# Rebuilding the head of a token, attention and expert kernel: bias exponentials, layer norm, load order and TensorE's order

## The reference, cut to what matters

```python
h = tok_embedding[x] + position_row                 # (2, 2048, 64)
a = layernorm(layernorm(h)) * ln1_g + ln1_b         # both norms, then q, k, v
q, k, v = split(a @ qkv_w + qkv_b, 3)
attn = softmax(q @ k.T + bias_table[m - n + 2047 clipped to 1022]) * scale
h = h + layernorm(attn @ v @ proj_w + proj_b) * ln2_g + ln2_b
g = layernorm(h);  top 2 of 8 experts by g @ Wg + bg + bias
h = h + sum over the two of weight * (relu(g @ W1[e] + b1[e]) @ W2[e] + b2[e])
```

## Time and profile before

| | us |
|---|---|
| median of 3 runs | 143.33 |
| the three runs | 142.25, 143.33, 146.63 |
| the profiled execution, its span from first to last instruction | 143.1 |
| DVE busy | 113.6 (79%) |
| PE busy | 106.9 (75%) |
| POOL busy | 71.6 (50%) |
| ACT busy | 59.4 (42%) |

### The profile page before, as it was taken

How to read it: one execution, slowest core, us unless ns; L and a number is a source line. 1 busy time by engine, 2 the same in 40 slices (tenths; PEclk the granted TensorE clock), 3 DMA queues, 4 the chain that set the end, 5 groups by cost and what they waited for, 6 DMA issues and landing times.

```text
span 143.1 us, 2799 instructions
## 1 busy us (share of the span) xinstructions
PE 106.9 (75%) x1029; PEld 61.7 (43%) x1029; DVE 113.6 (79%) x339; ACT 59.4 (42%) x114; POOL 71.6 (50%) x85
## 2 busy tenths in 40 slices
PE   0007655999989999999959759759747959729980
PEld 0003343459448547734623433625422446327650
DVE  6599999893955177169999998998999999999623
ACT  3005600210020464369968942647946625620020
POOL 2059991502620286256968993549399830360000
PEclk9999999999755558659999996986997576896555
DMA  3785000000000000000000000001000001004021
GB/s 82 285 321 216 0 0 0 0 5 1 5 0 0 0 0 0 0 2 7 0 0 7 0 0 0 5 5 32 0 5 2 0 8 33 0 0 110 5 73 37
DMA packets 5397, 4.45 MB, mean 31 GB/s; under 512 B 4515, under 2 KB 4743, under 8 KB 5256
## 3 DMA queue, kind: packets, MB, share of 16 engines
q1 hardware_dynamic: 5162, 4.18, 9.0%
q10 hardware_dynamic: 222, 0.10, 0.4%
HBM read 3.21 MB, written 1.06 MB: 30 GB/s over the span
## 4 chain that ended last, share of the span: by engine, by line
PE 44%; DVE 43%; issue 5%; DMA 3%; ACT 2%; POOL 1%; SPq 0%; DVEq 0%; ACTq 0%; POOLq 0%
PE bank L909 9%; DVE acc L818 6%; PE bank L1060 5%; PE bank L1080 4%; DVE prod L811 4%; PE bank L991 3%; DMA vec<-in_vecs_dram 3%; PE bank L988 3%; DVE xs L777 3%; PE bank L1075 2%; PE bank L1085 2%; DVE oneh_j L639 2%; DVE xs L776 2%; DVE xn L614 2%; PE bank L998 2%
## 5 line engine op out<-in xcount | busy, mean ns | idle before, releaser
L314 POOL TENSOR_TENSOR hid_lo<-hid,hid_hi 128x512 f16<-128x512 f32 (+1 forms) x38 | 41.9, 1118 | 17.3 <-ACT hid_hi L543 17.2
L543 ACT ACTIVATE hid<-bank,b_col 128x512 f32<-128x512 f32 (+1 forms) x40 | 25.8, 648 | 20.4 <-PE bank L1060 20.3
L543 ACT ACTIVATE hid_hi<-bank,b_col 128x512 f16<-128x512 f32 (+1 forms) x38 | 24.5, 645 | 0.0
L818 DVE TENSOR_REDUCE acc<-prod 128x64 f32<-128x512 f32 x18 | 18.6, 1034 | 0.4
L1060 PE MATMUL bank<-xT,w_hi 128*128 128x512 f16 (+1 forms) x40 | 17.3, 432 | 0.6 <-ACT hid_hi L543 0.6
L1060 PE MATMUL bank<-xT,w_lo 128*128 128x512 f16 (+1 forms) x40 | 17.5, 437 | 0.0
L811 DVE TENSOR_TENSOR prod<-bank,comb 128x512 f32<-128x512 f32 x18 | 12.4, 688 | 4.7 <-PE bank L1085 4.3
L442 POOL TENSOR_TENSOR rs<-var,neghalf 128x4 f32<-128x4 f32 (+1 forms) x5 | 4.8, 952 | 20.7 <-DVE var L755 20.6
L1080 PE MATMUL bank<-w_hi,hid_hi 128*128 128x64 f16 x144 | 13.3, 210 | 1.9 <-DVE hid_lo L314 1.9
L1080 PEld LDWEIGHTS bank<-w_hi,hid_hi 128*128 128x128 f16 x144 | 10.9, 108 | 7.4 <-issue 5.2
L1080 PE MATMUL bank<-w_lo,hid_hi 128*128 128x64 f16 x144 | 13.3, 210 | 0.0
(11 more groups left out here) (218 smaller groups left out, 228.1 us busy)
## 6 DMA issues: line engine op xcount, KB each, us to landing
ids_all<-ids_scratch SPq DMA_DIRECT2D x1, 1024.0 KB, 4.7
w_sb<-in_w1g_dram SPq DMA_DIRECT2D x1, 516.0 KB, 5.6
hankel<-in_bias_table_dram SPq DMA_DIRECT2D x1, 512.0 KB, 4.5
out_dram<-looked SPq DMA_DIRECT2D x2, 256.0 KB
table_all<-in_bias_table_dram SPq DMA_DIRECT2D x1, 511.5 KB, 5.0
out_dram<-fin_all SPq DMA_DIRECT2D x3, 128.0 KB
w_sb<-in_w2b_dram SPq DMA_DIRECT2D x1, 260.0 KB, 5.4
vec<-in_vecs_dram SPq DMA_DIRECT2D x1, 200.5 KB, 4.1
```

Source lines behind the costliest of these rows:

```text
L314: return eng.tensor_tensor(hid_lo[:, k % 2, e, 0:m], hid[:, n % HSLOTS, 0:m], hid_hi[:, k % 2, e, 0:m], ALU.subtract)
L543: ins = act.activation(dst, bank[n % 2][:, 0:m], ACT.Relu, bias=b1_col[:, e:e + 1], scale=HSCALE / (XSCALE * XSCALE))
L818: link(dve.tensor_reduce(acc[:, i, :], prod[:, n % 2].rearrange("p e d -> p d e"), AX.X, ALU.add))
```

## The change

- **Loads.** `table_all` goes; `table_part` (the table spread over 128 partitions, 8 entries each, 4 KB) takes its place. `hankel` is issued before the wait for token numbers. `vec` is loaded in two pieces on ACT's queue, the three rows of `hv` first. The broadcast of token numbers is split: late halves first.
- **Bias maximum.** DVE reduces 8 columns, PE turns the 128 maxima to one row, DVE reduces it, PE spreads the negated result with a matmul by ones.
- **Exponentials.** ACT writes `toe_hi` (f16) and `efull` (f32) straight from the reversed Hankel matrix, in two halves, with ln 32768 in the bias; DVE is left with one subtraction a half (`toeplitz_low`). POOL copies the constant parts.
- **One layer norm.** Two norms in a row are one with `var * (1 + eps) + eps * eps`; DVE subtracts and multiplies in one instruction a row kind.
- **One-hot blocks.** All 16 on DVE, in the order in which weights(0), weights(1) and the rest need them.
- **`skip_weights`.** One matmul for each block distance and part: 16 with 8 to 1 columns instead of 96 with one.
- **PE's order.** weights(0), counts, pair scores without penalties, `project_values`, weights(1) and `skip_weights` stand ahead of `pair_penalties`, which gives `s_g`. scores(1) comes right after scores(0); attend(2, 4) stands ahead of turn(0) and gate(0); scores(2) and weights(2, 0, 2) ahead of turn(1).
- **`bias_parts`** moves from DVE to POOL, behind `table_values` and ahead of rsqrt1(0).

```diff
-            sp.dma_start(vec[:], vecs.partition_broadcast(P)).then_inc(loads["vecs"], 16)
-            sp.dma_start(table_all[:], bias_table[0:TABLE].partition_broadcast(P)).then_inc(loads["table"], 16)
+            sp.dma_start(table_part[:], bias_table[0:1024].rearrange("(p c) -> p c", c=8)).then_inc(loads["table"], 16)
+            sp.dma_start(hankel[:], bass.AP(bias_table.tensor, 0, [[1, P], [1, 1024]])).then_inc(loads["hankel"], 16)
             sp.wait_ge(s_ids, 1)
             sp.dma_start(ids_dram.rearrange("s (r p) -> r s p", p=P), ids_b[:]).then_inc(loads["scratch"], 16)
-
-            sp.dma_start(hankel[:], bass.AP(bias_table.tensor, 0, [[1, P], [1, 1024]])).then_inc(loads["hankel"], 16)
             sp.wait_ge(loads["scratch"], 16)
-            sp.dma_start(ids_all[:, 0:SEQS * LEN],
-                         ids_dram.rearrange("s n -> (s n)").partition_broadcast(P)).then_inc(loads["ids_all"], 16)
+            ids_by_seq = ids_all[:, 0:SEQS * LEN].rearrange("p (s n) -> p s n", n=LEN)
+            sp.dma_start(ids_by_seq[:, :, FIRST:], ids_dram[:, FIRST:].partition_broadcast(P)).then_inc(loads["ids_late"], 16)
+            sp.dma_start(ids_by_seq[:, :, 0:FIRST], ids_dram[:, 0:FIRST].partition_broadcast(P)).then_inc(loads["ids_early"], 16)
...
             pool.wait_ge(s_const, 2)
-            for n in range(2):
-                pool.wait_ge(s_vvar, n + 1)
-                pool.tensor_tensor(vrs[:], vvar[:], neghalf[:, 0:3], ALU.pow).then_inc(s_vrs, 1)
-
-            pool.wait_ge(s_idcol, 1)
-            pool.wait_ge(s_ident, 1)
-            for c in range(BY_POOL):
-                pool.tensor_scalar(oneh_j[:, c, :], iota_h[:], id_col[:, c:c + 1], 0.0, ALU.is_equal, ALU.add).then_inc(s_onejp, 1)
+            pool.wait_ge(s_vvar, 1)
+            pool.tensor_tensor(vrs[:], vvar[:], neghalf[:, 0:3], ALU.pow).then_inc(s_vrs, 1)
+
+            pool.wait_ge(s_expb, 1)
+            pool.tensor_copy(toe_hi[:, 0:TOE_FLAT], toe_hi[:, TOE_FLAT:TOE_FLAT + 1].to_broadcast([P, TOE_FLAT]))
+            pool.wait_ge(s_toe, 1)
+            pool.tensor_copy(toe_lo[:, 0:TOE_FLAT], toe_lo[:, TOE_FLAT:TOE_FLAT + 1].to_broadcast([P, TOE_FLAT])).then_inc(s_flat, 1)
...
+            def bias_parts():
+                pool.wait_ge(loads["b2"], 16)
+                link(pool.tensor_scalar(b2_row[:], b2_row[:], YSCALE, 0.0, ALU.mult, ALU.add))
...
-            w1_parts(); table_values(); rsqrt1(0); rsqrt2(0); w2_parts(); rsqrt1(1); low(0, 0)
+            w1_parts(); table_values(); bias_parts(); rsqrt1(0); rsqrt2(0); w2_parts(); rsqrt1(1); low(0, 0)
...
+            act.dma_start(vec[:, 0:3 * D], vecs[0:3 * D].partition_broadcast(P)).then_inc(loads["hv"], 16)
             act.dma_start(w_tok[:], token_w).then_inc(loads["w_tok"], 16)
             act.dma_start(qkv_sb[:], qkv).then_inc(loads["qkv"], 16)
+            act.dma_start(vec[:, 3 * D:], vecs[3 * D:].partition_broadcast(P)).then_inc(loads["vecs"], 16)
             act.preload_act_table(ACT.Exp)
 
+            def table_exps(part):
+                cols = slice(HALF * part, HALF * (part + 1))
+                src = hankel[:, HALF * (1 - part):HALF * (2 - part)][:, ::-1]
+                act.activation(toe_hi[:, TOE_FLAT + HALF * part:TOE_FLAT + HALF * (part + 1)], src, ACT.Exp, bias=nbmax[:, 0:1])
+                act.activation(efull[:, cols], src, ACT.Exp, bias=nbmax[:, 0:1]).then_inc(s_expb, 1)
+
+            act.wait_ge(loads["hankel"], 16)
+            act.wait_ge(s_nbmax, 1)
+            table_exps(0)
             act.wait_ge(s_hT, 1)
             act.wait_ge(loads["qkv"], 16)
             act.activation(hvT[0:D, :], bank[2][0:D, 0:IDS], ACT.Identity, bias=qkv_sb[0:D, C_B1:C_B1 + 1],
                            scale=qkv_sb[0:D, C_G1:C_G1 + 1]).then_inc(s_hTsb, 1)
-
-            act.wait_ge(loads["hankel"], 16)
-            act.wait_ge(s_nbmax, 1)
-            act.activation(hankel[:], hankel[:], ACT.Exp, bias=nbmax[:, 0:1]).then_inc(s_expb, 1)
+            table_exps(1)
             act.wait_ge(s_qkv, 1)
...
-            count_late(0); count_late(1); read_v(); pair_exps(); read_turned_exps(); squares(0)
-            score_tile(0); read_turned(0); choice_exp(0); squares(1); hidden(0, 0); hidden(0, 1)
-            hidden(0, 2); hidden(0, 3); score_tile(1); hidden(0, 4); hidden(0, 5); squares(2)
-            read_turned(1); hidden(0, 6); hidden(0, 7); choice_exp(1); score_tile(2); hidden(1, 0)
+            read_v(); count_late(0); count_late(1); pair_exps(); read_turned_exps(); squares(0)
+            score_tile(0); score_tile(1); read_turned(0); choice_exp(0); squares(1); hidden(0, 0); hidden(0, 1)
+            hidden(0, 2); hidden(0, 3); hidden(0, 4); hidden(0, 5); squares(2)
...
+            dve.wait_ge(loads["table"], 16)
+            dve.tensor_reduce(tmax[:], table_part[:], AX.X, ALU.max).then_inc(s_tmax, 1)
...
-            row_stats(hv, vstat, vmv, vvar, 3, 1.0, EPS, s_vvar)
-            link(centre(vy[:], hv, vmv, 3))
-
+            for i in range(3):
+                ins = dve.bn_stats(vstat[:, i, :], hv[:, i, :])
+            dve.wait_ge(s_tmaxT, 1)
+            dve.tensor_reduce(ntop[:], bank[1][0:1, 0:P], AX.X, ALU.max, negate=True).then_inc(s_ntop, 1)
+            link(ins)
+            for i in range(3):
+                ins = dve.bn_aggr(vmv[:, i, :], vstat[:, i, :])
+            link(ins)
+            dve.tensor_scalar(vvar[:], vmv[:, :, 1], 1.0 + EPS, EPS * EPS, ALU.mult, ALU.add).then_inc(s_vvar, 1)
+            dve.wait_ge(s_ntops, 1)
+            dve.tensor_scalar(nbmax[:], bank[1][:, P:P + 1], LN_ESCALE, None, ALU.add).then_inc(s_nbmax, 1)
             dve.wait_ge(s_idT, 1)
             dve.tensor_copy(id_col[:], bank[0].bitcast(BF16)[:, 0:2 * ROWS]).then_inc(s_idcol, 1)
             dve.wait_ge(s_idcol, 1)
 
-
-            dve.wait_ge(loads["table"], 16)
-            dve.tensor_reduce(tmax[:, 0:1], table_all[:, 0:512], AX.X, ALU.max)
-            dve.wait_ge(s_vrs, 1)
-            link(rescale(vy[:], vy[:], vrs, 3))
-            row_stats(vy, vstat, vmv, vvar, 3, 1.0, EPS, s_vvar)
-            link(centre(vy[:], vy[:], vmv, 3))
-            link(dve.tensor_reduce(tmax[:, 1:2], table_all[:, 512:TABLE], AX.X, ALU.max))
-            dve.wait_ge(s_vrs, 2)
-            rescale(vy[:], vy[:], vrs, 3).then_inc(s_hl, 1)
-            link(dve.tensor_reduce(nbmax[:], tmax[:], AX.X, ALU.max))
-            dve.tensor_scalar(nbmax[:], nbmax[:], -1.0, None, ALU.mult).then_inc(s_nbmax, 1)
-            dve.tensor_scalar(skip_j[:], id_col[:, ROWS:2 * ROWS], float(SKIP_ID), None, ALU.is_equal)
-            def one_hot_rows():
-                for c in range(BY_POOL, SEQS * JBLK):
+            def one_hot_rows(c0, c1):
+                for c in range(c0, c1):
                     col = c // JBLK * ROWS + c % JBLK
                     ins = dve.tensor_scalar(oneh_j[:, c, :], iota_h[:], id_col[:, col:col + 1], None, ALU.is_equal)
                 ins.then_inc(s_onej, 1)
 
+            def spread_values():
+                dve.wait_ge(s_vrs, 1)
+                for i in range(3):
+                    ins = dve.tensor_scalar(vy[:, i, :], hv[:, i, :], vmv[:, i, 0:1], vrs[:, i:i + 1], ALU.subtract, ALU.mult)
+                ins.then_inc(s_hl, 1)
+
+            def skip_blocks():
+                dve.tensor_scalar(skip_j[:], id_col[:, ROWS:2 * ROWS], float(SKIP_ID), None, ALU.is_equal).then_inc(s_onej, 1)
...
+            def toeplitz_low(part):
+                cols = slice(TOE_FLAT + HALF * part, TOE_FLAT + HALF * (part + 1))
+                dve.wait_ge(s_expb, part + 1)
+                dve.tensor_tensor(toe_lo[:, cols], efull[:, HALF * part:HALF * (part + 1)], toe_hi[:, cols],
+                                  ALU.subtract).then_inc(s_toe, 1)
...
-                dve.tensor_reduce(sk_half[:, 0:1], skc[:, NQ:ROWS], AX.X, ALU.add)
-                dve.tensor_reduce(sk_half[:, 1:2], skc[:, 2 * NQ:ROWS], AX.X, ALU.add)
-                dve.tensor_reduce(sk_half[:, 2:3], skc[:], AX.X, ALU.add)
+                link(dve.tensor_tensor_scan(sk_suf[:, ::-1], skc[:, ::-1], skc[:, ::-1], 0.0, ALU.add, ALU.bypass))
+                dve.tensor_scalar(sk_flat[:], sk_suf[:, 1:1 + JBLK], flat, None, ALU.mult)
...
-            one_hot_rows(); late_one_hots(); toeplitz(); toeplitz_flat(); read_k(); read_counts()
-            penalties(); early_one_hots(); values(); flat_weights(); row_maxima(); skip_columns()
-            bias_parts(); split_exps(); rows_a(0); rows_b(0); rows_b2(0); skip_key(); rows_c(0)
-            key_part(0); skip_key_rows(); choose_a(0); choose_b(0); rows_a(1); rows_b(1); rows_b2(1)
-            key_part(1); rows_c(1); rows_a(2); choose_a(1); rows_b(2); rows_b2(2); weigh(0); key_part(2)
+            one_hot_rows(JBLK, JBLK + NQ); spread_values(); one_hot_rows(JBLK + NQ, 2 * JBLK); toeplitz_low(0)
+            one_hot_rows(0, JBLK); skip_blocks(); toeplitz_low(1); read_k(); late_one_hots(); read_counts()
```

(62 more changed lines are left out.)

112 lines of the change are left out of this document (55 added, 57 removed).

## The result

The changed kernel takes 146.79 us, median of 4 runs (145.79 to 148.58), beside 142.79 for the kernel before on the same chip (141.94 to 146.63): ratio 1.0277 [1.0151, 1.0403]. The forecast of 142.3 is wrong in sign, and 146.8 lies just above the range's 146.6. The profiled execution took 145.79 us with a span of 144.0.

What follows compares the result with a forecast made beforehand. It took a chain of waits as the bound: DVE to 23 us, PE to about 62, then mostly busy DVE. Unit 1's logits 0.9 earlier gave 143.1 - 0.9 = 142.2, with 0.2 to the median 142.3; range 137.8 to 146.6.

Steps and rivals of the forecast that it cites:

- Head up to q, k, v: Loads, maximum and the single norm ahead of the q, k, v matmuls: these start at 9.2 us against 12.53 before.
- To `s_g`: PE's unbroken row from q, k, v to the penalties, DVE no bound: `s_g` at 23.4 us, 2.6 earlier.
- Unit 1's attention end: From `s_g` through scores and attend(2, 4), 19.1 us: attention ends at 42.5 instead of 48.06, 5.6 gained.
- The choice behind attention: turn(0), gate(0) and choice now follow attend(2, 4): rows_a(1) at 45.8, only 2.8 earlier; PE idle ahead of embed(2).
- The logits of unit 1: End of the PE chain, after attend(6, 4) and 5.1 us more: logits at 61.1, 0.9 before 61.97.
- `bias_parts`, "Nothing, at worst 1": Six instructions moved from DVE to POOL, 3.0 to 6.4 us, ending at 25 to 29: costs nothing, at worst 1.
- "The rest of the span, 143.1 - 61.97 = 81.1 us, moves with it": All work behind unit 1's logits, left alone by the change, keeps its 81.1 us and shifts with the logits.
- "With the profiled execution 0.2 under the median": Step from span to median time: 0.2 us is added to 142.2, giving 142.3.
- Rival A: PE's clock stays up: `s_g` at 21.5, attend(6, 4) at the high clock again, 138.3 us; chance 0.27.
- Rival B: Slower, head stays at 1.2 GHz: `s_g` at 27.6, logits at 65.5, 146.6 us; chance 0.14.
- Rival C: The order costs nothing, hidden rows and choice fit beside PE's matmuls: 2.5 less, 139.8 us; chance 0.12.
- Rival D: `hankel` or `hv` land 1.5 us later than taken and PE starts late: 143.8 us; chance 0.07.

Runs made afterwards that it cites:

- e1: The changed kernel with turn(0) and gate(0) ahead of attend(2, 4) on PE: 144.79 us, ratio 1.0063 to the kernel before.
- e4: e1 with the order of before from attend(2, 4) on, only scores(1) kept early: 140.22 us, ratio 0.9851 to the kernel before.
- e2: The changed kernel with `bias_parts` moved from POOL back to DVE: 145.86 us, ratio 1.0113 to the kernel before.
- e5: The changed kernel with both the order of before and `bias_parts` on DVE behind choose_b(0): 138.23 us, ratio 0.9602 to the kernel before.
- e3: The changed kernel with the order of before on PE, ACT and DVE from scores(0) on: 139.36 us, ratio 0.9768 to the kernel before.
- r9: e5 run again without edit, in another group on its own chip: 139.48 us, ratio 0.968 to the kernel before.
- e0: The changed kernel run again without edit: 147.61 us, ratio 1.031 to the kernel before.
- The fill: The changed kernel with 13 added 512-column matmuls, results unused, where PE waits in unit 4: 144.74 us, ratio 0.9985 to the kernel before.

## Why the prediction was wrong

The steps in the order of the prediction:

- *Head up to q, k, v*: forecast 9.2, measured 9.38. weights(0) without waits at 12: measured 12.15. Right. (`vec` has 401 values, 200.5 KB, as the sum had it; the 513 in the description of the kernel is wrong.)
- *To `s_g`*: I had a rise at 13.6, a fall 3.1 later and `s_g` at 23.4. The rise came at 14.66 and held until about 24.9, so PE was faster than taken; DVE became the bound (0.86 waited for `absent_d`), since `sk_flat`, 128 x 8, took 2.17 us beside POOL's `w_lo`. "DVE's penalties are no bound" was wrong, at little cost: 22.3 against 23.4. (Two terms here are off as sums, without effect on the outcome: 13.6 + 3.1 + 4.4 is 21.1, not 21.4, and all at 2.4 GHz gives 19.8, not 20.2.)
- *Unit 1's attention end*: forecast 42.5, measured 42.40. Right, though the start at `s_g` was 1.1 earlier; the stretch between was 1.0 longer than forecast.
- *The choice behind attention*: rows_a(1) forecast 45.8, measured 45.73, right behind choose_b(0); idle time ahead of embed(2) over 2 us, measured 2.83. Right, and e1 confirms the cause.
- *The logits of unit 1*: forecast 61.1 (61.6 without the 0.4), measured 61.81. Nearly right. The level of the clock was as the rule against the change had it: 0.50 from the gap on, and none of the 0.4 came. The forecast had 5.1 from attention to logits where the kernel before needs 2.9; measured are 5.5, and e4, with the first layers and turn(1) placed as before, is back at 3.0.
- *`bias_parts`, "Nothing, at worst 1"*: this step failed. It ran 24.23 to 29.90 as bounded, but I asked only when POOL is done, not what DVE does meanwhile. DVE's one-hots, `gb_sum` and `deps` were held up: 1.2 us on the logits (e2), 2.5 with the better order (e5 against e3). The rows for it were there: the prediction itself says that a 2.13 us addition of 128 x 2 values ended with POOL's `w_lo`.
- *"The rest of the span, 143.1 - 61.97 = 81.1 us, moves with it"*: this is the step that failed and that made the wrong sign. The part behind the logits took 82.2 and 83.9 in the changed kernel's two profiles, 81.1 and 79.7 in those of the kernel before. I took PE's clock as a question of the head only, though the earlier trace rows gave 0.81 for 62 to 138.5 and showed the level swing in it (1.00, then 0.51), and I took one execution's tail for the kernel's.
- *"With the profiled execution 0.2 under the median"*: this reading is wrong, as is the sentence on what lies around the span in the section on the time before. A run's time was its span and 1.8 us more in every execution of these two kernels, so the profiled 143.1 was an execution of 144.9 us, 1.6 over the median. The forecast of the median doesn't depend on it (143.33 less 0.9 is 142.4; 142.2 and 0.2 is that too, not 142.3), but it hid that the 81.1 belonged to a slow execution.

Put together, the median of 146.79 is 61.81 to the logits, 83.2 behind them and 1.79 around the span; the forecast had 61.1, 81.1 and about 0.1. The forecast is short by 0.7, 2.1 and 1.7; the last two belong together, since the 81.1 was the tail of an execution above the median. For the kernel before, the same cut of its median beside it (142.79) gives 61.9, 79.1 and 1.8. So at the logits head and order cancel, and all of the rise of 4.0 is tail: 79.1 to 83.2. This takes the logits of the profiles for those of all executions, which r9 shows to hold only in part. Beside e0 to e3 the kernel before has the median 143.8, a tail of 80.1; against that the changed kernel's mean of 83.7 (145.5 - 61.8) is 3.6 longer.

What the longer tail is made of, the table of the tails shows for the profiles: 1.4 to 2.0 us in the last wait at the lower level, 1.0 where DVE is held beside POOL, and in the changed kernel's second profile another 1.1 ahead of unit 4's logits. The fill, which gives 2.5 to 3 back, supports the clock's part. The granted clock of the whole execution doesn't carry it: the changed kernel's slowest spans, 146.8 and 146.3, have 0.746 and 0.759, its fastest, 144.0, has 0.740. What stays open is why the changed kernel meets the poor end in all of its eight executions (spans 144.0 to 146.8), while the kernel before and e5 meet either (e5's four spans are 134.4 and 134.5, 138.4 and 138.8; tails of the profiles 79.6 to 80.8 in e3, e4 and e5, 83.4 in r9). e1 and e2, with most of the new order, have profiles with tails of 83.8, but e1 also has executions with a span of 140.2 to 141.0. The runs don't tell whether the length of the gaps decides or the moment at which they come.

Rival A (clock stays up) didn't come: the clock fell at 24.9. Rival B gave the right size, 146.6, for a cause that wasn't at work in either profile of the changed kernel; its nearness to the result is luck. Rival C (the order costs nothing) is refuted by e3 at 5.0 us on the logits, twice its price. Rival D is refuted by the DMA landings: `hankel` took 4.3 and `hv` was used at 4.29. A chance of 0.15 for slower was too low: the trace showed a net gain of 0.9 left from 5.6, with one term that could only lose left unpriced (POOL beside DVE) and the largest one, the tail, assumed constant.

## What to carry to other kernels

Shortening a head and reordering what follows are two changes: cost and run them apart. Here the same head is 2.3% faster with the old order (3.2% and 4.0% in two groups with `bias_parts` back on DVE too) and 2.8% slower with the new. When an early stage moves, look in every in-order queue at what now stands ahead of the first reader of the moved result; here `squares(2)` behind three hidden tiles cost 2.6 us, the choice behind attention 1.8. And where the clock is granted in swings, don't take the rest of the span as constant: take two profiles of the kernel before, place each among the runs, compare their tails, and hold that difference in the range. In the tail, look also at which small instructions of DVE will come to lie beside POOL's.

## What was not expected of the hardware

- POOL's small instructions cost DVE more than their size suggests. A 128 x 8 operation took 2.17 us (16.87 to 19.04) and ended with POOL's two-input 128 x 1032 `w_lo`. POOL's timeline, kernel after:

```profile
16.88 2.14 POOL L430 TENSOR_TENSOR w_lo<-w_sb,w_hi 128x1032 f16<-128x1032 f32 x1
...
25.73 1.20 POOL L454 TENSOR_TENSOR b_rest<-b_row,b_part 1x512 f32<-1x512 f32 x1
...
27.89 1.35 POOL L456 TENSOR_TENSOR b_rest<-b_rest,b_part 1x512 f32<-1x512 f32 x1
```

  Beside the two subtractions on a single partition, `gb_sum` (128 x 8) took 1.10 instead of 0.15 and `deps` 1.11 instead of 0.17. The Trainium skill, GPSIMD Engine Reference, 1. Specifications, says that POOL shares its SBUF interfaces with DVE, with contention for DVE instructions that have two SBUF inputs or run in a 2-port mode. `gb_sum`, with two inputs, agrees; in which mode `deps` and `sk_flat` ran, no run here shows. In the rows all three end within 0.03 us of POOL's instruction, also where that has one partition.
- The place of one rise of the clock in the head moved by at least 6.6 us between two executions of one kernel (e5 by 17.72, r9 at 24.35), and the logits by 3.4.
- Thirteen matmuls with unused results, in gaps of PE, made the run about 2.5 to 3 us shorter, though not at the wait that they were meant for.
- A run's time was its span and 1.8 us (1.75 to 1.87) in every execution of the kernels without fill. With fill it was 1.74 to 2.71.
